# One PSUM bank's order turned in a decoder layer's attention loop: query transposes back ahead of the next batch's projection

## The chip, the cores and the metric

The kernel runs on one core of a Trainium2 chip. The metric is device time in microseconds (us) of one execution; a run's time is compared with runs of the kernel before. TensorE's matmuls are called PE here, its weight loads PEld, VectorE DVE, ScalarE ACT, GpSimd POOL and SyncE SP, as the profile names them.

## The reference, cut to what matters

One decoder layer over a batch of 16 sequences, 128 tokens, 256 channels: self-attention with two softmaxes per head (16 heads of 16 channels, split in halves after the rotary turn), cross-attention of the same length, a mixture of 8 experts with two shared ones, and a layer norm after each. The change lies in the self-attention, and the order that it changes also holds steps of the cross-attention.

```python
qkv = x @ w_qkv.T
q, k, v = jnp.split(qkv, 3, axis=-1)
q = apply_rope(q, cos, sin); k = apply_rope(k, cos, sin)
q1, q2 = jnp.split(q, 2, axis=-1); k1, k2 = jnp.split(k, 2, axis=-1)
def sdpa(qh, kh):
    scores = jnp.einsum('bhqd,bhkd->bhqk', qh, kh) * scaler + add_mask
    p = jax.nn.softmax(scores, axis=-1)
    return jnp.einsum('bhqk,bhkd->bhqd', p, v)
out = sdpa(q1, k1) - lam * sdpa(q2, k2)
```

## The kernel before, in words

The kernel has two blocks. The first does both attentions and the router's logits, the second the experts and the last norm; the second begins when every engine is through with the first. The weights and activations go through PE as pairs of float16 numbers (a high part and what is left over), which is why a projection is six matmuls.

**The attention loop.** One iteration n of the first block works on several of the 16 batches at once, each at another stage. It projects batch n, makes the self-attention scores of batch n-1, the self-attention softmax and values of batch n-2, the output projection of n-3, cross-attention scores of n-3 and n-4, and so on down to the router of n-7. There are 23 iterations (line 62). Each engine has a `body(n)` that is a list of steps written out by hand (PE line 1031, ACT 528, DVE 774, POOL 389), and runs them in that order; engines meet only through semaphores. A step whose semaphore is not there yet holds up everything behind it on its engine.

**How one batch's scores are made.** Self-attention (A) and cross-attention (C) share the pattern. `project_qk` (line 881) projects queries and keys of A into PSUM. DVE makes the rotary turn in three passes that read that bank: `rope_second` (649, recorded at L651), `rope_first` (645, L647) and `rope_straight` (641, L643); each counts up the semaphore `s_rdve`. POOL adds the parts (`rope_sum`, 294, L297), ACT and POOL split them into high and low parts (`q_high` 450, `q_low` 299). Then PE transposes queries and keys (`stack_q` 904, `stack_k` 912, eight and eight half-size records at L901) into one bank, ACT or DVE copies them out (`qm_in`, `kt_in`: 1,024 float16 elements per partition, L488, L496 on ACT, L657 on DVE). A first round of scores (`max_scores`, L933) serves only to find each row's maximum (`largest` on DVE, 671, L675), which is written into a spare column of the query tile. PE transposes the queries again with that column (`restack`, 918, L901) and ACT (A) or DVE (C) copies them out (`reqt_in`, L502 on ACT). The second round (`exp_scores`, L944 for the mask, L950) gives the scores with the maximum taken off, which ACT turns into exponentials (`exp`, 505, L508). `values_self` (L964) and `values_cross` (L978) multiply by the values, `ot_in` (ACT, L514) copies the result out, and `back_T` (L988) turns it back. `group_mean` (L995) is a small matmul for a group norm, read by `group_out` (L725) on DVE.

**Banks and turns.** PSUM has eight banks. `RINGS` (line 50) names for each bank or pair of banks which results pass through it, in which order and for which batch; the second number is how many iterations behind n its batch is. `Turns.wait` (line 95) makes each PE step wait until the engine that reads the bank's previous occupant has read it: for "qk" the reader is DVE's third rotary pass (three counts of `s_rdve`), for "are" (the second query transposes of A) it is the copy `reqt_in`, for "xT" (batch n's inputs, transposed) it is `x_low`. The third ring is one bank, `a_one`, with six occupants per iteration:

```python
(1, (("aqT", 1, 0), ("akT", 1, 0), ("v", 1, 0), ("xT", 0, 0), ("qk", 0, 0), ("are", 1, 0))),
```

So before the change `restack` of batch n-1 waits for two things: the maxima of its batch, and the three rotary passes of batch n that read the bank.

The first ring, two banks, takes the `max_scores` of C and A in turn: C's rows 0 and 1 of an iteration's end, rows 2 to 7 in the next iteration's beginning. Row 2 of C may be written only when DVE has taken the maximum of row 0.

**The end of one iteration and the beginning of the next, on PE:** `max_scores(A, n-1, 7)`, `project_qk(n)`, `stack_q(C, n-3)`, `group_mean(n-2)`, `restack(A, n-1)`, `values_cross(n-4, 1)`, `max_scores(C, n-3, 0)` and `1`, `back_T(C, n-4, 0)`; then `exp_scores(A, 0)`, `max_scores(C, 2)`, `exp_scores(A, 1)`, `max_scores(C, 3)` and so on in turn. `stack_q(C)` waits for ACT's `kt_in(C)`, because the keys of C passed through its bank just before.

**On DVE, at the same place:** `largest(A, n-1, 7)`, `group_in_square`, `group_in_mean`, `rope_second(n)`, `spread(C)` (bn_stats, L701), `group_out`, `rope_first`, `cross_moments` (L761), `rope_straight`; then `largest(C, 0)` to `5` of the next iteration. **On ACT:** `kt_in(C)`, `exp(C, 6)`, `exp(C, 7)`, `qm_in(C)`, `ot_in(C, 0)`, `reqt_in(A)`; then `ot_in(C, 1)`, `exp(A, 0)`, `exp(A, 1)`, `q_high`, `k_high`. In iterations 1 to 3 ACT and DVE end with two pieces of the shared experts' weights each (`split_high` L211, `split_low` L218).

Of the kernel before, what the change touches and what calls it, by code (L numbers as in the profile page):

```python
# [53 lines left out]
    (2, (("ae", 2, 0), ("ae", 2, 1), ("ae", 2, 2), ("ae", 2, 3), ("ae", 2, 4), ("ae", 2, 5), ("ae", 2, 6),  # L54
         ("ae", 2, 7), ("ce", 4, 0), ("ce", 4, 1), ("ce", 4, 2), ("ce", 4, 3), ("ce", 4, 4), ("ce", 4, 5),
         ("ce", 4, 6), ("ce", 4, 7))),
    (1, (("aqT", 1, 0), ("akT", 1, 0), ("v", 1, 0), ("xT", 0, 0), ("qk", 0, 0), ("are", 1, 0))),
    (1, (("rt", 7, 0), ("cre", 4, 0), ("x2T", 6, 0), ("ckT", 3, 0), ("cqT", 3, 0))),
    (1, (("apv0", 2, 0), ("abk0", 2, 0), ("cpv0", 4, 0), ("cbk0", 4, 0))),
    (1, (("yT", 3, 0), ("cbk1", 5, 0), ("out", 3, 0), ("apv1", 2, 0), ("abk1", 2, 0), ("gm", 2, 0), ("cpv1", 4, 0))),  # L60
# [46 lines left out]
def build(nc, a, out):  # L107
    ctx = ExitStack()
    sems = ExitStack()
    with sems, ctx:  # L110
# [56 lines left out]
        A = attention_tiles("a_", HEADS)  # L167
        C = attention_tiles("c_", KV)
        a_one, c_one, a_out = ps[:, 4, :], ps[:, 5, :], ps[:, 7, :]
# [53 lines left out]
        def live(b):  # L223

            return 0 <= b < B
# [198 lines left out]
        def _(act):  # L424
# [74 lines left out]
            def reqt_in(t, one, b):  # L499

                act.wait_ge(t.s_reT, b + 1)
                act.activation(t.qt[:].rearrange("p c n -> p (c n)"), one.bitcast(F16), ACT.Copy  # L502
                               ).then_inc(t.s_reqt, 1)

            def exp(t, b, f):

                act.wait_ge(t.s_expfill, FILLS * b + f + 1)
                act.activation(t.pt[:, f, :, :].rearrange("p j n -> p (j n)"), score_bank(t, "e", b, f), ACT.Exp,  # L508
                               scale=(E // HEADS if t is A else SD) ** -0.5).then_inc(t.s_exped, 1)
# [18 lines left out]
            def body(n):  # L528

                if live(n - 5):  # L530
                    ot_in(C, n - 5, 1)
                if live(n - 2):
                    exp(A, n - 2, 0)
                    exp(A, n - 2, 1)
                if live(n - 1):
                    q_high(n - 1)
                    k_high(n - 1)
                if live(n - 2):
                    exp(A, n - 2, 2)
                    exp(A, n - 2, 3)  # L540
                if live(n - 3):
                    y_high(n - 3)
                if live(n - 2):
                    exp(A, n - 2, 4)
                    exp(A, n - 2, 5)
                    exp(A, n - 2, 6)
                if live(n - 1):
                    kt_in(A, a_one, n - 1)
                if live(n - 2):
                    exp(A, n - 2, 7)  # L550
                if live(n - 3):
                    cross_k_high(n - 3)
                if live(n - 2):
                    ot_in(A, n - 2, 0)
                    ot_in(A, n - 2, 1)
                if live(n - 4):
                    exp(C, n - 4, 0)
                    exp(C, n - 4, 1)
                if live(n - 1):
                    v_in(n - 1)  # L560
                if live(n - 4):
                    exp(C, n - 4, 2)
                    exp(C, n - 4, 3)
                if live(n - 6):
                    x2_high(n - 6)
                if live(n):
                    x_high(n)
                if live(n - 4):
                    exp(C, n - 4, 4)
                    exp(C, n - 4, 5)  # L570
                if live(n - 3):
                    cross_q_high(n - 3)
                    kt_in(C, c_one, n - 3)
                if live(n - 4):
                    exp(C, n - 4, 6)
                    exp(C, n - 4, 7)
                if live(n - 3):
                    qm_in(C, c_one, n - 3)
                if live(n - 4):
                    ot_in(C, n - 4, 0)  # L580
                if live(n - 1):
                    reqt_in(A, a_one, n - 1)

            body(0)
            setup()
# [9 lines left out]
        def _(dve):  # L595
# [23 lines left out]
            qk = a_one.rearrange("p (h d) -> p h d", d=HD)  # L619
# [13 lines left out]
            def rope_free(b):  # L633

                dve.wait_ge(A.s_qk, b + 1)
                if b == 0:
                    dve.wait_ge(s_const, 16 * N_CONST)
                else:
                    dve.wait_ge(A.s_klo, b)

            def rope_straight(b):

                dve.tensor_tensor(r1, qk, turned(cos[:]), ALU.mult).then_inc(A.s_rdve, 1)  # L643

            def rope_first(b):

                dve.tensor_tensor(rq[:, :, 0:SD], qk[:, :, SD:HD], turned(sin[:, 0:SD]), ALU.mult).then_inc(A.s_rdve, 1)  # L647

            def rope_second(b):

                dve.tensor_tensor(rq[:, :, SD:HD], qk[:, :, 0:SD], turned(sin[:, SD:HD]), ALU.mult  # L651
                                  ).then_inc(A.s_rdve, 1)
# [121 lines left out]
            def body(n):  # L774

                if live(n - 4):
                    largest(C, n - 4, 0)
                    largest(C, n - 4, 1)
                    largest(C, n - 4, 2)
                    largest(C, n - 4, 3)  # L780
                    largest(C, n - 4, 4)
                    largest(C, n - 4, 5)
                if live(n - 1):
                    qm_in(A, a_one, n - 1)
                if live(n - 3):
                    y_low(n - 3)
                if live(n - 4):
                    largest(C, n - 4, 6)
                    largest(C, n - 4, 7)
                if live(n - 7):  # L790
                    logits(n - 7)
                if live(n - 5):
                    cross_divide(n - 5)
                    cross_mix(n - 5)
                if live(n - 4):
                    reqt_in(C, c_one, n - 4)
                if live(n - 3):
                    add_self(n - 3)
                if live(n - 1):
                    largest(A, n - 1, 0)  # L800
                    largest(A, n - 1, 1)
                if live(n - 3):
                    spread(A, A.y2, A.bn2, n - 3, A.s_add, A.s_bn2)
                    moments(A, A.bn2, A.mv2, n - 3, A.s_bn2, A.s_mv2)
                if live(n - 1):
                    largest(A, n - 1, 2)
                    largest(A, n - 1, 3)
                if live(n - 2):
                    mix_divide(n - 2)
                    mix_lambda(n - 2)  # L810
                if live(n - 1):
                    largest(A, n - 1, 4)
                if live(n - 2):
                    mix_half(n - 2, 1)
                    mix_half(n - 2, 0)
                if live(n - 6):
                    x2_low(n - 6)
                if live(n - 1):
                    largest(A, n - 1, 5)
                if live(n):  # L820
                    x_low(n)
                if live(n - 2):
                    spread(A, A.y, A.bn, n - 2, A.s_y, A.s_bn)
                if live(n - 1):
                    largest(A, n - 1, 6)
                if live(n - 2):
                    moments(A, A.bn, A.mv, n - 2, A.s_bn, A.s_mv)
                if live(n - 1):
                    largest(A, n - 1, 7)
                if live(n - 2):  # L830
                    group_in_square(n - 2)
                    group_in_mean(n - 2)
                if live(n):
                    rope_free(n)
                    rope_second(n)
                if live(n - 5):
                    spread(C, C.y, C.bn, n - 5, C.s_y, C.s_bn)
                if live(n - 2):
                    group_out(n - 2)
                if live(n):  # L840
                    rope_first(n)
                if live(n - 5):
                    cross_moments(n - 5)
                if live(n):
                    rope_straight(n)

            body(0)
# [10 lines left out]
        def _(pe):  # L858
# [22 lines left out]
            def project_qk(b):  # L881

                pe.wait_ge(A.s_xlo, b + 1)
                if b == 0:
                    pe.wait_ge(s_set, 1)
                turns.wait(pe, "qk", b)
                split_matmul(a_one, x_hi, x_lo, lambda c: wq_hi[:, c, 0:2 * E],
                             lambda c: wq_lo[:, c, 0:2 * E], EC).then_inc(A.s_qk, 1)
# [142 lines left out]
            def body(n):  # L1031
# [79 lines left out]
                    exp_scores(C, n - 4, 7)  # L1111
                if live(n - 1):
                    max_scores(A, n - 1, 7)
                if live(n):
                    project_qk(n)
                if live(n - 3):
                    stack_q(C, c_one, n - 3)
                if live(n - 2):
# [2 lines left out]
                    restack(A, a_one, n - 1)  # L1121
                if live(n - 4):
                    values_cross(n - 4, 1)
                if live(n - 3):
                    max_scores(C, n - 3, 0)
                    max_scores(C, n - 3, 1)
# [3 lines left out]
            for n in range(ITERATIONS):  # L1130
                body(n)
# [710 lines left out]
```

## Time and profile before

| what | us |
|---|---|
| median of 3 runs (lowest to highest) | 874.15 (873.18 to 878.59) |
| the profiled execution, its own time | 873.48 |
| its span, from first to last instruction | 871.2 |
| iteration n = 3 to n = 4, by DVE's third rotary pass (86.95 to 117.76) | 30.81 |
| a later iteration (186.43 to 209.32) | 22.89 |
| end of the attention loop, start of the experts | about 457 |

A row of a timeline has the start in us from the span's start, the duration (of the whole run of instructions where several are merged), the engine, the line, what was written from what, the shape and the number of instructions; in square brackets how long the engine had been idle before it and which instruction of which engine ended that. PE's records overlap, since matmuls are pipelined: the next one starts before the one before has ended.

### The profile page before, as it was taken

What the parts mean: (1) busy time and instruction counts of PE and PEld (TensorE: products, weight loads), DVE (VectorE), ACT (ScalarE), POOL (GpSimd) and SP (SyncE); (2) the same over time, 40 slices, a digit from 0 to 9 for tenths busy, and PEclk for the clock granted to TensorE, in tenths of its full rate; (3) what the DMA queues carried; (4) which work ended last, traced back from release to release, by engine and by line L of the source; (5) the groups of instructions that cost most, each with busy time, mean ns of one, the idle gap of its engine ahead of it and who ended that gap; (6) DMA issues with size and microseconds to landing.
All of it is one profiled execution on the core that took longest, in us unless ns stands there. A gap on an engine that the chain in (4) does not pass through costs nothing. (4 is left out here: it accounts for less than half of the span.)

```text
span 871.2 us, 19681 instructions
## 1 busy us (share of the span) xinstructions
PE 773.9 (89%) x7471; PEld 503.0 (58%) x7471; DVE 520.7 (60%) x1182; ACT 520.2 (60%) x942; POOL 312.5 (36%) x481
## 2 busy tenths in 40 slices
PE   2879788999999999999868989998999999999993
PEld 1435455555555555555434545566788888887662
DVE  3445577777777778875525967675444444444353
ACT  2335577778777787877434545554555655555443
POOL 3123344555545554555420177000222222222222
PEclk9986699999999999999758999999999999999997
DMA  8109000000000000000003578351322332222231
GB/s 239 62 1 281 17 2 2 3 2 2 2 2 2 2 2 2 2 2 2 1 1 94 162 241 239 123 168 32 50 45 49 50 48 46 50 45 49 44 115 60
DMA packets 38280, 50.98 MB, mean 59 GB/s; under 512 B 9264, under 2 KB 33072, under 8 KB 38192
## 3 DMA queue, kind: packets, MB, share of 16 engines
q1 hardware_dynamic: 31040, 40.39, 15.6%
q0 software_dynamic: 7152, 9.34, 6.4%
q8 instruction: 64, 1.05, 0.5%
q14 instruction: 24, 0.20, 0.1%
HBM read 31.04 MB, written 18.68 MB: 57 GB/s over the span
## 5 line engine op out<-in xcount | busy, mean ns | idle before, releaser
L1326 POOL DMA_INDIRECT acc<-y_sb,xin x39 | 60.5, 1552 | 219.0 <-ACT y_sb L1394 219.0
L1647 PE MATMUL ps<-wr,xr_hi 128*128 x624 | 129.3, 299 | 0.0
L1365 ACT ACTIVATE th<-ps 128x384 f32<-128x384 f32 (+1 forms) x118 | 57.9, 491 | 113.4 <-PE ps L1647 108.5
L1647 PE MATMUL ps<-xg_hi,wsh 128*128 128x512 f16 x320 | 104.4, 389 | 4.8 <-DVE xg_lo L1512 4.8
L675 DVE TENSOR_REDUCE c_qs<-ps 128x4 f16<-128x512 f32 x128 | 83.5, 693 | 37.3 <-PE ps L933 35.7
L675 DVE TENSOR_REDUCE a_qs<-ps 128x4 f16<-128x512 f32 x128 | 85.4, 691 | 23.9 <-PE ps L933 22.9
L508 ACT ACTIVATE a_pt<-ps 128x512 f32<-128x512 f32 x128 | 74.7, 595 | 41.8 <-PE ps L950 39.5
L1647 PE MATMUL ps<-wr,xr_lo 128*128 x312 | 93.4, 299 | 0.0
L1519 DVE SCALAR_TENSOR_TENSOR th<-th,ps 128x384 f32<-128x384 f32 (+1 forms) x118 | 65.3, 554 | 36.9 <-ACT th L1365 36.8
L508 ACT ACTIVATE c_pt<-ps 128x512 f32<-128x512 f32 x128 | 69.8, 604 | 19.8 <-PE ps L950 19.5
L1606 DVE COPY ht<-ps 128x512 f16<-128x512 f16 x39 | 16.6, 425 | 93.7 <-PE ps L1726 93.7
L1647 PE MATMUL ps<-wr,ht 128*128 x585 | 70.4, 273 | 0.7 <-issue 0.7
L1647 PEld LDWEIGHTS ps<-wr,xr_hi 128*128 128x128 f16 x624 | 59.4, 98 | 18.2
L1647 PE MATMUL ps<-xg_lo,wsh 128*128 128x512 f16 x160 | 62.4, 390 | 0.0
L1647 PEld LDWEIGHTS ps<-wr,ht 128*128 128x128 f16 x585 | 56.9, 98 | 8.2 <-issue 1.4
L944 PE MATMUL ps<-mask,id 128*128 128x512 f16 x128 | 54.4, 425 | 4.3 <-ACT a_qt L502 3.0
L1647 PE MATMUL ps<-wsh,ht_hi 128*128 128x256 f16 x320 | 54.6, 273 | 3.7 <-DVE ht_lo L1524 3.6
L1647 PEld LDWEIGHTS ps<-xg_hi,wsh 128*128 128x128 f16 x320 | 32.0, 100 | 41.6 <-issue 8.6
L1524 DVE TENSOR_TENSOR hs<-th,hs 128x384 f16<-128x384 f32 x78 | 38.4, 492 | 29.0 <-ACT hs L1370 29.0
L1370 ACT ACTIVATE hs<-th 128x384 f16<-128x384 f32 x78 | 36.6, 470 | 31.9 <-DVE th L1519 31.9
L950 PE MATMUL ps<-a_qt,a_kt 32*128 32x128 f16 x512 | 55.2, 233 | 0.0
L950 PEld LDWEIGHTS ps<-a_qt,a_kt 32*128 32x128 f16 x512 | 31.1, 99 | 37.1 <-issue 37.1
(209 smaller groups left out, 1736.2 us busy)
## 6 DMA issues: line engine op xcount, KB each, us to landing
wst<-in_wx SPq DMA_DIRECT2D x30, 640.0 KB, 4.6
xs<-zero SPq DMA_DIRECT2D x1, 5031.0 KB, 24.6
xin<-xs SPq DMA_DIRECT2D x39, 129.0 KB, 2.1
acc<-x_row SPq DMA_DIRECT2D x4, 512.0 KB, 3.6
x_row<-acc SPq DMA_DIRECT2D x8, 256.0 KB, 5.5
out<-x_row SPq DMA_DIRECT2D x8, 256.0 KB, 2.1
x_row<-in_x SPq DMA_DIRECT2D x1, 1536.0 KB, 10.4
wst<-in_wqkvT SPq DMA_DIRECT2D x1, 768.0 KB, 4.2
```

The costliest lines, as they stand in the source:

```text
L508: act.activation(t.pt[:, f, :, :].rearrange("p j n -> p (j n)"), score_bank(t, "e", b, f), ACT.Exp, scale=(E // HEADS if t is A else SD) * ...
L675: dve.tensor_reduce(t.qs[:].rearrange("p (c i) s -> p c i s", i=NI)[:, c:c + 4, f % 4, USED], score_bank(t, "m", b, f).rearrange("p (j n) ...
L944: pe.matmul(o.rearrange("p (j n) -> p j n", j=NI), id16[:], mask4[:].unsqueeze(1).to_broadcast([P, NI, P]), start=True, stop=False, skip_g ...
L950: ins = pe.matmul(o[:, j * P:(j + 1) * P], t.kt[r, c, :], t.qt[r, c, :], start=t is C, stop=True, skip_group_check=t is A)
L1326: pool.indirect_dma_start(acc, bass.IndirectOffsetOnAxis(ap=row, axis=0), y_sb[:, n % 2, :], None, compute_op=ALU.add).then_inc(f_acc, 16)
L1365: act.activation(th[:, k % 2, 0:n], gate[:, k % 2, 0:n], ACT.Silu, scale=1.0 / WSCALE).then_inc(f_th, 1)
L1370: act.activation(dst, th[:, k % 2, 0:dst.shape[-1]], ACT.Copy).then_inc(f_hhi, 1)
L1519: dve.scalar_tensor_tensor(out=t, in0=t, scalar=1.0 / WSCALE, in1=up[:, k % 2, 0:n], op0=ALU.mult, op1=ALU.mult).then_inc(f_hid, 1)
L1524: dve.tensor_tensor(dst, th[:, k % 2, 0:dst.shape[-1]], hi, ALU.subtract).then_inc(f_hlo, 1)
L1606: dve.tensor_copy(ht[:, HALVES[1][0]:, :, :].rearrange("p j r n -> p (j r n)"), htp[1]).then_inc(f_hTin[1], 1)
L1647: ins = pe.matmul(o, l[x], r[y], start=(first and n == 0), stop=(last and n == m - 1), skip_group_check=not (first and last))
```

## The change

It changes three lists. In the ring of bank `a_one`, "are" and "qk" trade places. PE's `project_qk(n)` moves from ahead of `stack_q(C)` to behind `values_cross(n-4, 1)`. On DVE, `spread(C)`, `group_out` and `cross_moments` come ahead of the three rotary passes, which then follow each other as the last steps of the iteration. On ACT, `reqt_in(A)` moves from the iteration's last place to ahead of `qm_in(C)` and `ot_in(C, 0)`. No instruction is added or taken away, none changes its shape. By the ring, `restack(A, n-1)` now waits for its maxima and for `x_low(n)`; `project_qk(n)` waits for `reqt_in(A, n-1)`.

```diff
-    (1, (("aqT", 1, 0), ("akT", 1, 0), ("v", 1, 0), ("xT", 0, 0), ("qk", 0, 0), ("are", 1, 0))),
+    (1, (("aqT", 1, 0), ("akT", 1, 0), ("v", 1, 0), ("xT", 0, 0), ("are", 1, 0), ("qk", 0, 0))),
@@ ACT body @@
+                if live(n - 1):
+                    reqt_in(A, a_one, n - 1)
                 if live(n - 3):
                     qm_in(C, c_one, n - 3)
                 if live(n - 4):
                     ot_in(C, n - 4, 0)
-                if live(n - 1):
-                    reqt_in(A, a_one, n - 1)
@@ DVE body @@
+                if live(n - 5):
+                    spread(C, C.y, C.bn, n - 5, C.s_y, C.s_bn)
+                if live(n - 2):
+                    group_out(n - 2)
+                if live(n - 5):
+                    cross_moments(n - 5)
                 if live(n):
                     rope_free(n)
                     rope_second(n)
-                if live(n - 5):
-                    spread(C, C.y, C.bn, n - 5, C.s_y, C.s_bn)
-                if live(n - 2):
-                    group_out(n - 2)
-                if live(n):
                     rope_first(n)
-                if live(n - 5):
-                    cross_moments(n - 5)
-                if live(n):
                     rope_straight(n)
@@ PE body @@
                 if live(n - 1):
                     max_scores(A, n - 1, 7)
+                if live(n - 3):
+                    stack_q(C, c_one, n - 3)
+                if live(n - 2):
+                    group_mean(n - 2)
+                if live(n - 1):
+                    restack(A, a_one, n - 1)
+                if live(n - 4):
+                    values_cross(n - 4, 1)
                 if live(n):
                     project_qk(n)
-                if live(n - 3):
-                    stack_q(C, c_one, n - 3)
-                if live(n - 2):
-                    group_mean(n - 2)
-                if live(n - 1):
-                    restack(A, a_one, n - 1)
-                if live(n - 4):
-                    values_cross(n - 4, 1)
```

## Rows read from the trace of the kernel before

**Rows 1.** The page, part 1: busy time of each engine.

```profile
PE 773.9 (89%) x7471; PEld 503.0 (58%) x7471; DVE 520.7 (60%) x1182; ACT 520.2 (60%) x942; POOL 312.5 (36%) x481
```

**Rows 2.** Busy time by stretch, granted clock (PEclk): iterations 2, 3 and a later one.

```profile
core 0: us, PE busy (x) PEld busy (x) DVE busy (x) ACT busy (x) POOL busy (x), PEclk, DMA share, GB/s
...
59.76:86.95 27.19, 23.15 (x176) 12.82 (x176) 13.44 (x32) 14.83 (x24) 11.82 (x18) 0.69 0.80 225
86.95:117.76 30.81, 24.23 (x256) 14.30 (x256) 19.55 (x41) 19.23 (x33) 12.04 (x19) 0.72 0.05 14
...
186.43:209.32 22.89, 20.83 (x280) 12.73 (x280) 18.00 (x46) 18.08 (x34) 11.98 (x22) 1.00 0.01 1
```

**Rows 3.** Whom PE waited for, 140.7 to 369.5 us: total, times, longest.

```profile
PE ps L901 <- DVE a_r L643: 13.9, 10, 1.4
PE ps L933 <- DVE a_qs L675: 3.7, 10, 0.4
```

**Rows 4.** Timeline of all engines across one iteration's end, 183.7 to 190 us.

```profile
183.74 1.02 ACT L496 ACTIVATE c_kt<-ps 128x1024 f16<-128x1024 f16 x1 [0.68 <-PE ps L950]
...
183.75 0.39 PE L875 MATMUL ps<-wq_hi,a_xt_hi 128*128 128x512 f16 x1
...
184.66 1.08 ACT L508 ACTIVATE c_pt<-ps 128x512 f32<-128x512 f32 x2
...
184.84 0.38 PE L875 MATMUL ps<-wq_hi,a_xt_lo 128*128 128x512 f16 x1
...
185.26 0.43 DVE L651 TENSOR_TENSOR a_rq<-ps,sin 128x256 f32<-128x256 f32 x1 [0.52 <-PE ps L875]
185.60 0.42 DVE L701 BATCH_NORM_STATS2 c_bn<-c_y 128x6 f32<-128x256 f32 x1
...
186.43 0.66 DVE L643 TENSOR_TENSOR a_r<-ps,cos 128x512 f32<-128x512 f32 x1
...
187.23 0.61 PE L901 MATMUL ps<-id,a_qs 128*128 128x128 f16 x8 [1.39 <-DVE a_r L643]
...
187.88 1.02 ACT L502 ACTIVATE a_qt<-ps 128x1024 f16<-128x1024 f16 x1 [0.66 <-PE ps L901]
...
188.77 0.41 PE L933 MATMUL ps<-c_kt,c_qm 24*128 24x128 f16 x8
...
189.20 2.59 DVE L675 TENSOR_REDUCE c_qs<-ps 128x4 f16<-128x512 f32 x4 [2.11 <-PE ps L933]
...
189.60 0.38 PE L944 MATMUL ps<-mask,id 128*128 128x512 f16 x1
...
189.95 0.22 PE L933 MATMUL ps<-c_kt,c_qm 24*128 24x128 f16 x1
```

**Rows 5.** Timeline of PE at the end of iteration 16, which projects nothing.

```profile
390.88 0.61 PE L901 MATMUL ps<-id,c_qs 128*128 128x128 f16 x8 [1.09 <-ACT c_kt L496]
391.32 0.34 PE L995 MATMUL ps<-a_ge,grp 128*128 128x2 f32 x2
391.51 0.61 PE L901 MATMUL ps<-id,a_qs 128*128 128x128 f16 x8
392.05 1.07 PE L978 MATMUL ps<-c_pt,c_v 128*32 128x512 f32 x8
393.05 0.41 PE L933 MATMUL ps<-c_kt,c_qm 24*128 24x128 f16 x8
```

**Rows 6.** Timeline of ACT at the same place in iteration 16.

```profile
389.71 1.02 ACT L496 ACTIVATE c_kt<-ps 128x1024 f16<-128x1024 f16 x1 [0.76 <-PE ps L950]
390.63 1.08 ACT L508 ACTIVATE c_pt<-ps 128x512 f32<-128x512 f32 x2
```

**Rows 7.** Timeline of PE after iterations 1 and 3, the first with the mask.

```profile
33.80 0.61 PE L944 MATMUL ps<-mask,id 128*128 128x512 f16 x1 [1.11 <-ACT a_qt L502]
...
36.60 0.61 PE L944 MATMUL ps<-mask,id 128*128 128x512 f16 x1 [0.58 <-ACT a_pt L508]
...
94.19 0.60 PE L933 MATMUL ps<-c_kt,c_qm 24*128 24x128 f16 x4 [3.77 <-DVE c_qs L675]
```

More of the change, by code:

```diff
@@ L832, in body @@
                     group_in_mean(n - 2)
-                if live(n):
-                    rope_free(n)
-                    rope_second(n)
                 if live(n - 5):
@@ L839, in body @@
                     group_out(n - 2)
-                if live(n):
-                    rope_first(n)
                 if live(n - 5):
@@ L844, in body @@
                 if live(n):
+                    rope_free(n)
+                    rope_second(n)
+                    rope_first(n)
                     rope_straight(n)
@@ L1113, in body @@
                     max_scores(A, n - 1, 7)
-                if live(n):
-                    project_qk(n)
                 if live(n - 3):
@@ L1123, in body @@
                     values_cross(n - 4, 1)
+                if live(n):
+                    project_qk(n)
                 if live(n - 3):
```

## The prediction

> **What bounds the kernel now.** I read the page first: PE is busy for 89% of the span, no other engine for more than 60% [rows 1]. Then the busy time by stretch, cut at the end of DVE's third rotary pass: an iteration takes 22.9 us, PE is busy for 20.8 of them and DVE and ACT for 18 each, at a granted clock of 1.00 (the last of these rows stands for the twelve iterations 4 to 15, which agree) [rows 2]. So in this loop PE's own order is the bound, and what counts are PE's pauses. The table of waits over ten such iterations names the largest: `restack(A)` waits 1.39 us each time (13.9 us in ten) for L643, the third rotary pass; next comes 0.37 us for a maximum [rows 3]. The timeline shows how it arises [rows 4]: `project_qk` runs on PE from 183.75, its last matmul ends at 185.22, DVE begins the rotary turn at 185.26 and ends it at 187.09, and `restack` starts at 187.23. In the same rows DVE then idles for 2.11 us, until 189.20, when C's first scores are there and `largest(C, 0)` begins; PE's next step that needs it, `max_scores(C, 2)`, starts at 189.95, 0.06 us after that maximum (189.20 + 0.69).
>
> The change takes away the wait of 1.39 us. But what stood before `restack` also covered something, and what stood beside idle time of DVE now stands in front of its work. So I walk the new order through the iteration of rows 4, whose beginning up to 183.75 is as before.
>
> **The change part by part.**
>
> *The projection as a cover.* From 183.75 to 185.06 PE ran `project_qk`, six matmuls 0.22 us apart. `stack_q(C)`, next in line now, needs `kt_in(C)`, which ACT ends at 183.74 + 1.02 = 184.76 [rows 4]. Iteration 16 has no projection and shows this order: PE idles 1.09 us for that copy, and starts 0.15 us after its end (389.71 + 1.02 = 390.73 against 390.88) [rows 5, 6]. So `stack_q(C)` starts at 184.76 + 0.15 = 184.91, where without the copy it could at 183.75; behind it stand `group_mean`, `restack` and `values_cross`. With the spacings of iteration 16 (0.44, 0.19, 0.54 and 1.00 us [rows 5]) `group_mean` starts at 185.35, `restack` at 185.54, `values_cross` at 186.08, and PE is through with it at 187.08. `restack` is 1.69 us earlier than before.
>
> *The copy as a new wait.* `project_qk` must wait for `reqt_in(A)`, in the same bank. `restack` ends at 185.54 + 0.61 = 186.15, ACT starts 0.04 us later (as 187.23 + 0.61 = 187.84 against 187.88 [rows 4]), at 186.19; it is free by then, its exponentials end at 185.74. The copy takes 1.02 us, to 187.21, and with 0.15 us again `project_qk` starts at 187.36, 0.28 us after PE is free. Behind it wait `max_scores(C, 0)`, `1` and `back_T`. The delay from the copy to a matmul I bound by 0 and 0.15 us and take 0.15, as it was at `stack_q(C)`.
>
> *The rotary turn, which lost its cover.* From first to last matmul `project_qk` takes 1.09 us, the last lasts 0.38, DVE starts 0.04 later [rows 4]: 187.36 + 1.51 = 188.87. The three passes, now back to back, cost 0.34 each for the two halves (185.26 to 185.60) and 0.60 to 0.66 for the third: 1.28 to 1.34 us. `largest(C, 0)`, next on DVE, starts at about 190.15 where it did at 189.20: **0.95 us later**. These passes filled idle time of DVE before; now six maxima of C are queued behind them.
>
> *What of this PE feels.* Its matmuls for C's rows 0 and 1 start after the projection (187.36 + 1.30 = 188.66, before 188.77), and the mask of `exp_scores(A, 0)` about 0.1 us earlier than before. `qm_in(C)` and `ot_in(C, 0)`, pushed behind the copy on ACT, start 0.92 us after their forerunners (as 389.71 and 390.63 [rows 6]): at 187.11 and 188.03. They end near 188.1 and 188.6 (1.02 for such a copy, about 0.6 for one of 512 elements), in time for PE. But `max_scores(C, 2)` waits for `largest(C, 0)`: 190.15 + 0.69 + 0.06 = 190.90 against 189.95. PE is in order, so all that follows is 0.95 us late. Could later slack give it back? The later waits of PE in an iteration, 0.37 us for a maximum among them [rows 3], are on work that itself hangs on PE's earlier steps, and move along. So is the next batch's query path: `rope_sum` now starts at 190.2 and ends at 191.5, `q_high` sits on ACT behind `exp(A, 1)`, whose scores are also 0.95 late; the path has that much room and no more, so nothing is added. Per iteration I take +0.95 us, with 0.80 (copy to matmul at 0) and 1.1 (0.15 us once more at the rotary turn, with the third pass at its full 0.66) as bounds.
>
> *The ends.* Iteration 1 has no C and half-speed matmuls. There `restack` no longer waits for the projection, so the copy and ACT's two weight pieces behind it start earlier; PE loses the 0.58 us of waiting for ACT's exponentials and about half of its 1.11 us in front of the mask at 33.80 [rows 7]: -1.1 us, bounds -1.7 (both waits) and 0. In iteration 2 both orders come out about even: 0, bounds -1 and +1. In iteration 3 PE waits 3.77 us for C's maximum behind DVE's weight pieces [rows 7]; the rotary passes end later there, but those pieces wait for ACT's halves anyway, till nearly the same time: +0.4, bounds 0 and 0.95 (the full delay). In iteration 16 only ACT's order counts: `reqt_in(A)` runs from 392.16 to 393.18 ahead of `qm_in(C)`, which ends at 394.10, so C's first scores start at 394.25 instead of 393.05 [rows 5]: +1.2, bounds 0.5 and 1.5.
>
> **The sum.** Iterations 4 to 15 are twelve: 12 x 0.95 = 11.4. With -1.1, 0, +0.4 and +1.2: **+11.9 us**. The second block starts when the first ends and moves as a whole. The profiled execution took 873.48 us (span 871.2 and 2.3 around it), so 885.4; the median of the runs is 0.7 above that execution, so I forecast 886.0. By the bounds it is 12 x 0.80 - 1.7 - 1 + 0 + 0.5 = 7.4 to 12 x 1.1 + 0 + 1 + 0.95 + 1.5 = 16.7 us, that is 881.6 to 890.9 for the median.
>
> *A rule of the skill.* The row says that PE's pause falls on a bank whose reader is late, before the change DVE (1.39 us), after it ACT (1.02 us of copy). The Trainium skill, Perfetto Trace Analysis, section Matmuls, says that independent groups should pass through different banks so that emptying one overlaps the next group's matmuls. By that rule no order within one bank is free, and turning it changes only which emptying stands bare; the row agrees as far as the first order goes. It changes no term of the sum.
>
> **The rivals.**
>
> *B, the pause simply goes (faster).* If PE could go straight from A's last scores to `stack_q(C)` and `restack`, and the rotary turn fitted into DVE's 2.11 idle us, each of the twelve iterations would lose its 1.39: 873.5 - 16.7 - 1.1 = 855.7. For it: the idle 2.11 is longer than 1.3. Against it: iteration 16, where PE stands for the copy of C's keys [rows 5]; it decides whether that copy ends before 183.75 or, as now, at 184.76, and whether `project_qk` ends before about 187.8. The Trainium skill, Perfetto Trace Analysis, section Optimization Strategy, tells one to take the gaps of the most contended engine and make what they wait for come sooner; by it B is what to expect, and no row here shows the gap closing.
>
> *C, the late maxima cost nothing (no change).* If C's maxima had slack, PE alone would count: 1.16 us for the keys' copy and 0.28 for `reqt_in` against 1.39 plus the 0.1 us after it, about -0.1 per iteration; 873.5 - 1.2 + 0.5 = 873. Against it: `max_scores(C, 2)` follows `largest(C, 0)` by 0.06 us today [rows 4].
>
> *D, the clock falls too (much slower).* Iterations 2 and 3 show 0.69 and 0.72 of the full clock with PE busy for 23.15 of 27.19 and 24.23 of 30.81 us, the later ones 1.00 at 20.8 of 22.9 [rows 2]. The new order has PE pausing three times, together about 2.2 us instead of 1.39. If one stretch in each third iteration fell to 1.2 GHz, at some 4 us each (30.81 less 22.90 and less the 3.77 us of rows 7), it would be four of them: 886 + 16 = 902; one alone gives 890. In the same way the early stretches could come out quicker by 4. The Trainium skill, TensorE: Matmul & The Clock Gate, Part 1, says that the throttled state is the default and activity lifts it, so that pauses can bring it back; by that rule D is what more pauses lead to, and iterations 2 and 3 agree, though no row shows a pause of 1 us doing it.
>
> **How the numbers follow.** The forecast 0.74, B 0.08, C 0.10, D 0.08. Some 1% (8.7 us) is what a measurement of this kernel can tell from no change: 865.4 and 882.9 are the bounds. The forecast's lower end, below 882.9, is worth 0.02 of its 0.74; so slower 0.74 - 0.02 + 0.08 = 0.80, within 1% 0.10 + 0.02 = 0.12, faster 0.08. The range of 878 to 892 holds the forecast's bounds and the mild half of D, and leaves out B, C and the rest of D, about 0.2.
>
> **What would show it.** In the changed profile an iteration takes 23.8 us by DVE's third pass. PE's table of waits no longer has L901 for L643, but L901 for ACT L496 with about 1.1 us each, the projection (L875) for ACT L502 with 0.2 to 0.3, and L933 for DVE L675 with 0.7 to 1.0 more than now; DVE goes from L643 into L675 without a pause, and idles about 2.5 us before L651 instead. The forecast is wrong if `stack_q(C)` starts without that wait, if iterations stay at 22.9 or fall to 21.5, or if the clock in iterations 4 to 15 is not 1.00.

## The result, and the profile after

The changed kernel is slower, and by far more than forecast: 905.87 us (899.49 to 910.92, four runs) against 873.66 (869.75 to 878.59), a ratio of 1.036 with a 95% interval of 1.027 to 1.045. Run again beside other kernels it had 1.031 (1.026 to 1.035). The forecast was 886.0 with a range of 878 to 892: the side was right, the size was not. Its profiled execution took 908.13 us, with a span of 905.9.

First the page, busy time and the clock in 40 slices:

```profile
span 905.9 us, 19681 instructions
...
PE 794.9 (88%) x7471; PEld 511.3 (56%) x7471; DVE 525.1 (58%) x1182; ACT 519.0 (57%) x942; POOL 315.2 (35%) x481
...
PEclk9866588996899999999975999999999999999997
```

The granted clock of the kernel before, in 40 slices of its own span:

```profile
PEclk9986699999999999999758999999999999999997
```

The instructions are the same in number as in [rows 1]. PE is busy for 21 us longer with the same work, and PEclk dips in slices 6, 7, 10 and 11 (113 to 159 and 204 to 249 us), where the kernel before has no dip: both are signs of matmuls at the lower clock.

The loop is cut here at the starts of DVE's copy `qm_in(A)` (L657), a step that did not move. One full-clock stretch of the kernel before, cut like that, and then the changed kernel's, columns as in [rows 2]:

```profile
262.28:285.16 22.88, 20.82 (x281) 12.73 (x280) 17.98 (x45) 18.05 (x35) 12.09 (x23) 1.00 0.01 3
```

```profile
132.50:160.70 28.20, 25.54 (x273) 15.02 (x272) 17.88 (x43) 17.73 (x32) 10.53 (x21) 0.80 0.01 1
160.70:185.14 24.44, 21.89 (x281) 12.88 (x280) 18.15 (x44) 17.58 (x33) 11.62 (x21) 0.97 0.01 2
185.14:210.16 25.02, 22.58 (x281) 13.62 (x280) 18.09 (x45) 18.41 (x35) 12.94 (x25) 0.93 0.01 2
210.16:238.71 28.55, 26.12 (x281) 15.30 (x280) 18.29 (x45) 17.89 (x33) 11.54 (x22) 0.80 0.01 1
238.71:264.82 26.11, 23.57 (x281) 13.87 (x280) 18.22 (x46) 17.59 (x33) 11.81 (x21) 0.90 0.01 2
264.82:288.62 23.80, 21.25 (x281) 12.76 (x280) 18.04 (x46) 17.89 (x35) 12.02 (x23) 1.00 0.01 2
...
383.83:407.63 23.80, 21.26 (x281) 12.77 (x280) 18.04 (x46) 17.89 (x35) 12.14 (x23) 1.00 0.01 2
```

At the granted clock of 1.00 an iteration takes **23.80 us**, 0.92 more than the 22.88 before; the walk had said 0.95. But five of the eleven stretches from `qm_in(A)` of iteration 5 to that of iteration 16 were not at 1.00 (0.80 to 0.97), and took up to 28.55 us; the other six took 23.80.

PE's table of waits in the changed kernel, 140 to 370 us, answers to [rows 3]:

```profile
PE ps L899 <- ACT c_kt L496: 9.8, 9, 1.1
PE ps L931 <- DVE c_qs L675: 5.3, 9, 0.6
PE ps L931 <- DVE a_qs L675: 3.6, 9, 0.6
PE ps L873 <- ACT a_qt L502: 1.9, 9, 0.2
```

(The lines of PE's steps are two lower than before.) The wait for the rotary turn is gone, and three stand in its place: for the copy of C's keys (1.09 us), for the copy `reqt_in(A)` (0.21) and for C's first maximum (0.59, where the forecast had 0.7 to 1.0). The timeline of one full-clock iteration's end answers to [rows 4]; 94.09 us lie between them, as 277.83 is the counterpart of 183.74:

```profile
277.83 1.02 ACT L496 ACTIVATE c_kt<-ps 128x1024 f16<-128x1024 f16 x1 [0.68 <-PE ps L948]
...
279.00 0.61 PE L899 MATMUL ps<-id,c_qs 128*128 128x128 f16 x8 [1.09 <-ACT c_kt L496]
279.44 0.34 PE L993 MATMUL ps<-a_ge,grp 128*128 128x2 f32 x2
279.64 0.61 PE L899 MATMUL ps<-id,a_qs 128*128 128x128 f16 x8
...
280.28 1.02 ACT L502 ACTIVATE a_qt<-ps 128x1024 f16<-128x1024 f16 x1 [0.45 <-PE ps L899]
...
281.45 0.38 PE L873 MATMUL ps<-wq_hi,a_xt_hi 128*128 128x512 f16 x1 [0.21 <-ACT a_qt L502]
...
282.94 0.42 DVE L651 TENSOR_TENSOR a_rq<-ps,sin 128x256 f32<-128x256 f32 x1 [2.83 <-PE ps L873]
...
283.67 0.38 PE L942 MATMUL ps<-mask,id 128*128 128x512 f16 x1
...
284.21 1.29 DVE L675 TENSOR_REDUCE c_qs<-ps 128x4 f16<-128x512 f32 x2
```

Less 94.09 these are `stack_q(C)` at 184.91 (walk: 184.91), `restack` at 185.55 (185.54), `project_qk` at 187.36 (187.36), the rotary turn at 188.85 (188.87) and `largest(C, 0)` at 190.12 (190.15). Step for step the walk was right at the full clock.

**Where the 34.7 us between the two profiled spans lie**, cut by the same copy and by the experts' first copy out of PSUM (L1357 before, L1355 after):

```
stretch                              before   after   more
start to qm_in(A) in iteration 1      17.92   18.69   0.8
to qm_in(A) in iteration 5           107.04  113.80   6.8   (forecast 0.3)
to qm_in(A) in iteration 16          251.73  275.13  23.4   (forecast 10.5)
to the experts' first copy            82.12   82.30   0.2   (forecast 1.2)
the experts                          412.4   415.9    3.5   (forecast 0)
```

Of the 23.4 us, 11 x 0.92 = 10.1 are the longer iteration and 13.3 the lower clock. So three things were left out or mis-sized: the lower clock between iterations 5 and 16, 6.5 us in the early iterations, and some 4 us at both ends of the execution.

### The profile page after: what moved, and what is told of

Its sections match the earlier page's. It is cut to its first block and busy times, and to the rows that moved or that the text cites. A ratio compares the mean times of both kernels' runs of the same rounds, so it can differ in the third digit from the quotient of the medians.

```text
span 905.9 us, 19681 instructions
## 1 busy us (share of the span) xinstructions
PE 794.9 (88%) x7471; PEld 511.3 (56%) x7471; DVE 525.1 (58%) x1182; ACT 519.0 (57%) x942; POOL 315.2 (35%) x481
## 5 line engine op out<-in xcount | busy, mean ns | idle before, releaser
L942 PE MATMUL ps<-mask,id 128*128 128x512 f16 x128 | 57.9, 452 | 0.1
L948 PE MATMUL ps<-a_qt,a_kt 32*128 32x128 f16 x512 | 57.6, 240 | 0.0
```

What stands on the lines that cost most here:

```text
L942: pe.matmul(o.rearrange("p (j n) -> p j n", j=NI), id16[:], mask4[:].unsqueeze(1).to_broadcast([P, NI, P]), start=True, stop=False, skip_g ...
L948: ins = pe.matmul(o[:, j * P:(j + 1) * P], t.kt[r, c, :], t.qt[r, c, :], start=t is C, stop=True, skip_group_check=t is A)
```

## The experiments

Theory **P** was that PE's new pauses bring its clock down, theory **N** that its falls come from elsewhere. All kernels ran beside the kernel before on the same chip.

**1. Fill PE's pauses.** Matmuls that nobody reads in the two longest pauses of the changed kernel.

```diff
                 if live(n - 1):
                     max_scores(A, n - 1, 7)
+                if live(n) and live(n - 3):
+                    pe.wait_ge(A.s_xlo, n + 1)
+                    for _ in range(5):
+                        pe.matmul(a_one, id16[:], wq_hi[:, 0, 0:2 * E], start=True, stop=True)
...
                     exp_scores(A, n - 2, 0)
+                    if live(n - 1) and live(n - 2):
+                        turns.wait(pe, "ae", n - 2, 1)
+                        for _ in range(3):
+                            pe.matmul(score_bank(A, "e", n - 2, 1).rearrange("p (j n) -> p j n", j=NI), id16[:],
+                                      mask4[:].unsqueeze(1).to_broadcast([P, NI, P]), start=True, stop=True)
```

> The changed kernel, with PE's pauses filled by matmuls that nobody reads: five of 512 columns ahead of stack_q(C) (bank a_one, overwritten by restack) and three of the mask between exp_scores(A, 0) and max_scores(C, 2), in the iterations with self-attention and cross-attention (3 to 15). They fit into the pauses of 1.09 and 0.59 us, so at the full clock an iteration should stay at 23.8 us under both theories. Theory P (PE's pauses bring the clock down): the clock stays at 1.00 from iteration 4 on, no iteration there is above 24.0, and the time is 885 to 893. Theory N (the falls come from elsewhere, from the beginning or by chance): iterations 5 to 9 again contain some of 25 to 29 us, and the time is 900 to 915.

Measured: 890.46 us (889.72 to 890.58), less by doing more: 15 us below the changed kernel's first runs and 11 below its repeat (experiment 8). Every stretch from `qm_in(A)` of iteration 5 on took 23.9 us at 1.00; here two of them, with PE busy for 23 of 23.9 us:

```profile
200.51:224.42 23.91, 23.02 (x289) 13.38 (x288) 18.15 (x45) 17.89 (x35) 12.05 (x23) 1.00 0.01 2
224.42:248.32 23.90, 23.02 (x289) 13.37 (x288) 18.14 (x45) 17.89 (x35) 12.18 (x23) 1.00 0.01 2
```

That is P, not N: with the pauses filled the clock does not fall there. The filling takes a pause away and adds work on PE in one stroke, so these runs do not say which of the two keeps the clock up.

**2. One pause of the same sum.** The kernel before, with a longer wait for the third rotary pass.

```diff
+        scr = sb('scr', [P, 3 * E])
...
                 if live(n):
+                    if live(n - 3):
+                        dve.tensor_tensor(scr[:, 0:2 * E].rearrange("p (h d) -> p h d", d=HD), qk, turned(cos[:]),
+                                          ALU.mult)
+                        dve.tensor_tensor(scr[:, 2 * E:3 * E].rearrange("p (h d) -> p h d", d=SD), qk[:, :, SD:HD],
+                                          turned(sin[:, 0:SD]), ALU.mult)
                     rope_straight(n)
```

> The kernel before, with two more DVE instructions ahead of the third rotary pass (a copy of the third and one of the first pass, into a tile that nobody reads), some 0.95 us, in iterations 3 to 15. PE then has one pause of about 2.3 us per iteration instead of 1.39, where the changed kernel has three of 1.09, 0.2 and 0.59; an iteration at the full clock takes 22.88 + 0.95 = 23.8 us in both. Theory P by the sum of pauses (some 2.3 against 1.9 us): the clock falls in iterations 4 to 15 here too, 895 to 915. Theory P by their number and place: clock 1.00 from iteration 4 on and 884 to 888. Theory N: as by chance, either.

Measured: 887.53 us (885.59 to 889.10), iterations of 23.82 us. The waits, and one stretch with clock and busy time:

```profile
PE ps L907 <- DVE a_r L644: 23.2, 10, 2.3
...
220.92:244.73 23.81, 20.83 (x281) 12.74 (x280) 18.91 (x47) 18.05 (x35) 12.10 (x23) 1.00 0.01 2
```

PE is busy for 20.83 of 23.81 us here, less than the 21.25 of the changed kernel, with one pause of 2.3 us, and the clock held in ten of eleven stretches. In the other (25.15 us, between `qm_in(A)` of iterations 14 and 15) it fell once, inside the wait of 2.3 us. So it is not the sum of PE's pauses that told the two apart, nor the length of an iteration, which is 23.8 us in both; but one long pause is not quite harmless either.

**3. Each filling alone.** 

> The changed kernel with only the five unread matmuls ahead of stack_q(C), which fill the longest pause (1.09 us); the pause of 0.59 us in front of max_scores(C, 2) stays. If the longest pause alone brings the clock down: 1.00 from iteration 5 on, 888 to 892 like with both filled. If each pause counts: some iterations of 25 to 29 us between the fifth and the ninth, 893 to 905.

> The changed kernel with only the three unread matmuls in front of max_scores(C, 2), which fill the pause of 0.59 us; the pause of 1.09 us ahead of stack_q(C) stays. If the longest pause alone counts: 900 to 910 with iterations of 25 to 29 us, as without any filling. If each pause counts: fewer of these, 893 to 900.

With the long pause filled (1.09 us, ahead of `stack_q(C)`) the time was 907.87 us, as without filling; six of eleven stretches were longer than 23.8, up to 28.51 us. With only the short one filled (0.59 us, in front of `max_scores(C, 2)`) it was 895.22 us in two runs (891.67 and 898.78), and in the profile all eleven stretches took 23.90. Neither expectation had this case, in which the short pause alone matters; that 895.22 lies in the range given for "each pause counts" is luck. The profiles say the same together: in the three with that pause filled (this one, the first experiment, the sixth) none of 33 such stretches was slower; in the six with it open (the changed kernel twice, the long one filled, the fourth, fifth and seventh experiment) 28 of 66 were, from one to seven in a profile.

The place of the falls says it too. From `qm_in(A)` of iteration 4 to that of iteration 16 these six profiles have 72 waits of 0.59 us in front of `max_scores(C, 2)`, and the clock fell 22 times, by the trace's record of it: each time 1.1 to 3.1 us after the end of such a wait, and never elsewhere in the iteration. So that wait is followed by a fall often, but by no means always; why in some iterations and not in others stays open. One of the falls, in the changed kernel, 1.2 us after the wait's end (the last rows give the clock of the stretches around it, 1.00, 0.50 and 1.00):

```profile
205.29 0.39 PE L931 MATMUL ps<-c_kt,c_qm 24*128 24x128 f16 x4 [0.59 <-DVE c_qs L675]
...
200.00:206.40 6.40, 5.60 (x58) 2.70 (x59) 3.42 (x9) 3.71 (x7) 3.55 (x9) 1.00 0.00 0
206.50:219.90 13.40, 13.40 (x106) 7.87 (x106) 7.40 (x15) 6.88 (x13) 4.09 (x8) 0.50 0.00 1
220.20:237.10 16.90, 14.47 (x201) 8.29 (x193) 11.77 (x32) 12.48 (x23) 8.14 (x17) 1.00 0.01 2
```

**4. The copy back in its last place on ACT.**

```diff
-                if live(n - 1):
-                    reqt_in(A, a_one, n - 1)
                 if live(n - 3):
                     qm_in(C, c_one, n - 3)
                 if live(n - 4):
                     ot_in(C, n - 4, 0)
+                if live(n - 1):
+                    reqt_in(A, a_one, n - 1)
```

> The changed kernel, with reqt_in(A) back at the end of ACT's list. Then the copy starts behind qm_in(C) and ot_in(C, 0), at 187.26 instead of 186.19 in the iteration walked through, and project_qk, the rotary passes and largest(C, 0) follow it: by the walk an iteration at the full clock takes 23.8 + 1.0 = 24.8 us. If the copy is not on the path that sets an iteration (rival C), 23.8. The time is that of the changed kernel plus 12 for twelve iterations, or more if the clock falls oftener.

Measured: 921.06 us, and 24.65 us per full-clock iteration. PE's wait for the copy grew from 0.2 to 1.1 us:

```profile
PE ps L873 <- ACT a_qt L502: 9.5, 9, 1.1
```

So the copy is on the path, at nearly its full shift (0.85 of 1.0). PE's own wait for the copy grew by the same 0.85, so this does not tell whether the late maxima count. Rival C is out by the changed kernel itself: it had the iteration stay at some 22.8 us, and that is 23.80, with a wait of 0.59 for C's maximum that was not there before.

**5. The early iterations.** In the changed kernel PE waits 2.5 us for `q_low` after iteration 1. The timeline of POOL and DVE there:

```profile
35.59 2.44 POOL L297 TENSOR_TENSOR a_rq<-a_rq,a_r 128x512 f32<-128x512 f32 x1 [17.49 <-DVE a_r L643]
...
35.43 3.96 DVE L218 SCALAR_TENSOR_TENSOR wsh<-wst,wsh 128x1280 f16<-128x1280 f32 x2
```

`rope_sum` takes 2.44 us instead of 1.26, and DVE's two weight pieces 3.96 instead of 2.89, where they run side by side. Before, the rotary turn was over earlier, and in iterations 2 and 3 the pieces met `group_norm` on POOL, for which no engine is listed as waiting. So the pieces were moved to where POOL has nothing large:

```diff
                 if live(n - 1):
                     qm_in(A, a_one, n - 1)
+                if 2 <= n <= NSH * 3 // 2 + 1:
+                    for k in range(2):
+                        e, m = divmod(2 * n - 4 + k, 3)
+                        split_low(dve, 2 * n - 4 + k, k, wsh[:, e, m, 1, :], wsh[:, e, m, 0, :])
...
                 body(n)
-                if n <= NSH * 3 // 2:
-                    for k in range(2):
-                        e, m = divmod(2 * n - 2 + k, 3)
-                        split_low(dve, 2 * n - 2 + k, k, wsh[:, e, m, 1, :], wsh[:, e, m, 0, :])
```

> The changed kernel with DVE's weight pieces (L218) of iterations 1 to 3 moved into the next iteration, behind qm_in(A), where POOL has no large instruction. In the changed kernel rope_sum on POOL took 2.44 us instead of 1.26 and the two pieces 3.95 instead of 2.89 where they ran side by side, in these three iterations. If that collision made the early loss (2.5 us of waiting for q_low in iteration 1, and the iterations up to the fourth longer by 6.8 together than before): rope_sum is back at 1.26, and qm_in(A) of iteration 4 starts 4 to 6 us earlier than in the changed kernel (132.5 minus about 125.7 as before, at 127 to 128.5); the time is that of the changed kernel less 4 to 6. If it came from the clock alone: rope_sum shorter, but that start within 2 us of 132.5.

The instructions of `rope_sum` (shortest, median, longest in ns), in the changed kernel, then with the pieces moved:

```profile
L297 POOL TENSOR_TENSOR a_rq<-a_rq,a_r x16: 1259/1262/2443, 14.7 to 403.4; 128x512 f32<-128x512 f32 x16
```

```profile
L297 POOL TENSOR_TENSOR a_rq<-a_rq,a_r x16: 1259/1262/1264, 14.0 to 385.5; 128x512 f32<-128x512 f32 x16
```

`qm_in(A)` of iteration 5 (the fifth copy; the expectation counts by its batch, 4) starts at 122.65 us, 9.8 earlier than in the changed kernel and 2.3 earlier than before. In the profile of experiment 6, with the same move, it starts at 126.56; in the seven profiles of the changed order that leave the pieces in place, at 128.80 to 132.82. So the place of the pieces is the early loss, give or take some 4 us from profile to profile. The collision itself shows in the first stretch, from `qm_in(A)` of iteration 1 to 2, where PE's mask matmuls take 0.61 us instead of 0.38, so run at the lower clock, in the kernel before, in the repeat of the changed kernel (experiment 8) and in this one: 21.90 us before, 22.34 changed, 20.70 with the pieces moved. It costs 1.64 there, and without it the order gains 1.20, about the 1.1 that the forecast had for iteration 1. How much of the rest is collision and how much a lower clock in iterations 2 to 4 was not separated.

The time is 890.38 us (882.89 to 901.68), a ratio of 1.014 (1.0085 to 1.0196); in the profile the first of the eleven stretches is at the lower clock (29.07 us), and the ten behind it take 23.80, with the pause of 0.59 us still open.

**6. Both away.** The filling in front of `max_scores(C, 2)` and the moved pieces together, on the changed kernel.

> The changed kernel with both additions that the forecast had not counted taken away: three unread matmuls in front of max_scores(C, 2), after which the iterations from the fifth on ran at the full clock in one profile, and the weight pieces of iterations 1 to 3 behind the next qm_in(A). If these two make up what the change cost beyond the forecast: iterations of 23.9 us from the fifth on, and a time between the forecast's bounds less what the early iterations gain by the moved pieces, 879 to 886. If something else is left: 890 or more with every iteration at 23.9.

Measured: 884.48 us (880.58 to 893.25), a ratio of 1.0145 (1.010 to 1.019); every stretch from iteration 5 on 23.90 us. That is what the forecast had for the change alone (+11.9 us, a ratio of 1.0136), but not quite the same thing: moving the pieces helps the order of before too (below), so a part of the size is made up by luck. Nor can the runs tell what the filling adds once the pieces are moved: without it the ratio was 1.014 (experiment 5).

**7. The keys' copy out of the way of `restack`.**

```diff
+                if live(n - 1):
+                    restack(A, a_one, n - 1)
                 if live(n - 3):
                     stack_q(C, c_one, n - 3)
                 if live(n - 2):
                     group_mean(n - 2)
-                if live(n - 1):
-                    restack(A, a_one, n - 1)
```

> The changed kernel with restack(A) ahead of stack_q(C) and group_mean on PE, so that it needn't wait for ACT's copy of C's keys. By the walk reqt_in(A) is then held by ACT's exponentials, till 185.74 instead of 186.19 in the iteration walked through, and project_qk by values_cross, which waits for the group mean and ends at about 187.2 instead of 187.36: an iteration of 23.6 to 23.7 us instead of 23.8. If the wait for the keys' copy set the iteration (its 1.09 us): 22.7 us. The clock may fall as in the changed kernel, so the iteration at the full clock is what is read, not the time.

Measured: 23.65 us per full-clock iteration (897.91 us in all). The keys' copy was PE's longest wait and yet little of the price; behind it stood the wait of `restack(A)` for its own last maximum (0.8 us), the exponentials on ACT and the group mean. PE's waits now:

```profile
PE ps L899 <- DVE a_qs L675: 7.9, 10, 0.8
PE ps L931 <- DVE c_qs L675: 5.3, 9, 0.6
```

The second row, the price of the bare rotary turn, has not moved.

**8. The changed kernel again.** 

> The changed kernel once more, for a second profile of it. If the iterations at the lower clock have a fixed place: again the fifth to the ninth. If they come by chance with pauses of this kind: some of the iterations 4 to 15, others than before, at 24.4 to 29.4 us, and the rest at 23.8; 899 to 911.

Measured: 901.04 us (896.62 to 918.71). Its profile, of the slowest of these five executions (918.7 us), has six longer stretches, with two of them late (25.02 and 28.51 us at the very end) where the first profile ran at 23.80. So the falls have no fixed iteration; the profile with the long pause filled (experiment 3) has late ones too. The eleven stretches together take 276.8 us here and 275.1 in the first profile: what makes this execution longer lies behind the loop, 90.9 instead of 82.3 us up to the experts' first copy.

**9. Another filling for the wait of before.** `values_cross` does not need the rotary turn, so it can stand in that pause.

```diff
+                if live(n - 4):
+                    values_cross(n - 4, 1)
                 if live(n - 1):
                     restack(A, a_one, n - 1)
-                if live(n - 4):
-                    values_cross(n - 4, 1)
```

> The kernel before, with values_cross(n-4, 1) ahead of restack(A) on PE: it fills 1.0 us of the 1.39 us for the third rotary pass. C's first scores, and with them largest(C, 0), come 1.0 us earlier; the mask of exp_scores(A, 0) then waits for reqt_in(A), which stays where it was and ends at 188.90 in the iteration shown, so the mask starts at 188.96 instead of 189.60. By the walk through the rows an iteration takes 22.88 - 0.64 = 22.24 us, twelve of them gain 7.7: 866 if the clock stays. If C's late maxima don't count (rival C) the same. Theory P: fewer pauses, so the clock is not below that of before (0.947).

Measured: 867.90 us, a ratio of 0.9933 (0.9915 to 0.9952), 22.23 us per iteration. PE's waits there, where the 1.39 us for the rotary turn is 0.4 for the group mean and 0.2 for the copy:

```profile
PE ps L978 <- DVE a_g L725: 3.8, 10, 0.4
PE ps L933 <- DVE a_qs L675: 3.7, 10, 0.4
PE ps L944 <- ACT a_qt L502: 2.1, 11, 0.2
```

**10. With the weight pieces moved as well** (the edits of 9 and 5 on the kernel before). 

> The kernel before with values_cross ahead of restack (867.9 measured, an iteration 22.23 us) and with DVE's weight pieces of iterations 1 to 3 in the next iteration behind qm_in(A). There the pieces ran beside group_norm on POOL (L366, 3.42 instead of 0.87 us), and PE waited 3.77 us for C's maxima behind them in iteration 3. If the pieces stood in the way: group_norm at 0.87 us throughout, and 2 to 4 us less than with values_cross alone, 864 to 866. If the clock of the early iterations decides: within 2 us of 867.9.

Measured: **863.02 us** (860.69 to 866.44), a ratio of 0.9864 (0.9838 to 0.9890): faster than both kernels. `group_norm` on POOL, in the kernel before and in this one:

```profile
L366 POOL TENSOR_SCALAR a_yn<-a_y,a_gsc,a_gbi x32: 437/438/3025, 63.2 to 414.1; 128x128 f32<-128x128 f32 x32
```

```profile
L366 POOL TENSOR_SCALAR a_yn<-a_y,a_gsc,a_gbi x32: 438/444/448, 63.3 to 403.7; 128x128 f32<-128x128 f32 x32
```

Not tried: DVE's old order in the changed kernel. `group_out` would stand behind a rotary pass that waits for `project_qk`, which stands behind `values_cross`, which waits for `group_out`.

## Why the prediction was wrong

*The walk.* The term of 0.95 us per iteration was right: 0.92 measured, with its stations within 0.03 us, and the same kind of walk gave 22.24 for 22.23 (experiment 9), 23.6 to 23.7 for 23.65 (7) and 24.8 for 24.65 (4). Rival B fell, as its condition did: `stack_q(C)` waits for the keys' copy, 1.09 us, as iteration 16 had shown. Rival C fell with the iteration of 23.80 us.

*The step that failed* is the one that set rival D apart from the forecast: that the clock of iterations 4 to 15 would stay at 1.00, with 0.08 for the other case, priced at 4 us a stretch. It fell in five of eleven stretches of the profile for 13.3 us, and every run was above the range; the prediction had this among its own signs of being wrong. The reason given for D, the sum of the pauses (2.2 us for 1.39; measured 1.09 + 0.21 + 0.59 = 1.89), was not the right one either: a single pause of 2.3 us left the clock alone in ten of eleven stretches (experiment 2). What decided was the pause of 0.59 us in front of C's third row (experiments 1, 3, 6). That D's 902 comes near the measured time is partly luck: it had four falls of 4 us, and there were five stretches longer by 2.7 us on average and some 9 us more in the early iterations and at the ends. D should have been part of the likeliest case: the same rows that priced the late maximum showed where PE would stand still, and iterations 2 and 3 of the kernel before showed that this loop does lose its clock.

*The early terms.* Iteration 1 was put at -1.1, iteration 2 at 0 and iteration 3 at +0.4, with one 0.95 more up to the cut: 0.3 in all, against 6.8 measured. The step that failed is "the copy and ACT's two weight pieces behind it start earlier": that was so, but it let DVE's pieces begin right behind the rotary turn, 0.16 us before `rope_sum` on POOL, and the two hold each other up (experiment 5), 1.64 us in the first stretch. The lower clock of iterations 2 to 4, which varies from profile to profile, is the likely rest, and that is not shown. The kernel before had a row of it that I passed over, `group_norm` at 3.0 us for 0.44. Of a step that moves, what runs beside it on the other engines has to be listed too, not only what waits for it.

*The ends.* The +1.2 us of iteration 16 came out as 0.2 by the time the experts began, but that stretch took 82.30 us in one profile of the changed kernel and 90.92 in the other, so its size cannot be read there. The first copy began 0.8 us later; over all profiles of these kernels it began at 17.92 to 18.69, which looks like chance. The experts took 3.5 us longer: 415.9 in both profiles of the changed kernel, 410.0 to 413.2 in the eleven others, among them small variants of the same order. Why stays open.

## What to carry to other kernels

Turning two occupants of one bank did not remove a wait here; it chose which copy out of the bank stands bare, and what the old order had covered on other engines would have needed a new cover. The long wait was better filled with a step that needs none of the bank (experiment 9) than moved. And a kernel whose PE is busy for nine tenths of a loop can still lose its clock to a short pause in the wrong place, at a price larger than the pause: take such a fall into the range, and look in a second profile before you blame an iteration.

## What the runs showed of the hardware

The clock went from 2.4 to 1.2 GHz (granted 1.00 to 0.50 in the rows of experiment 3) in iterations with pauses of 1.09, 0.21 and 0.59 us, each time shortly after the last of them; with one of 2.3 us it fell once in eleven stretches, and it did not fall when the 0.59 was filled and the 1.09 left. Which part of PE's activity makes that difference is open: filling the long pause, with five matmuls against three, did not help. The Trainium skill, TensorE: Matmul & The Clock Gate, section A second HAM failure mode: psum-queue depth-cycling, tells of a kernel that swung between the levels because PE idled briefly and often; this trace agrees (five of eleven stretches), and the experiments add that it matters which pause is filled.

DVE's weight pieces (L218, two inputs in SBUF) and a POOL instruction hold each other up when side by side: `rope_sum` 1.26 to 2.44 us and two pieces 2.89 to 3.96 in the changed kernel, `group_norm` 0.44 to 3.03 with the pieces at their 2.89 before. The Trainium skill, SBUF — State Buffer, section Who interferes with whom, says that a DVE instruction with two inputs in SBUF contends with a POOL instruction that reads SBUF, and that contention between these engines is an exclusive lock. The trace agrees: `rope_sum` and the pieces together took 3.96 us, nearly what they take one after the other (1.26 + 2.89 = 4.15).
